# Attention kernel on one core: the projections of the next unit issued as four single products at steps 6, 8, 11 and 13 of a head, with their preparation one to two steps later

## What is computed

```
q = x @ W_q ; k = x @ W_k ; v = x @ W_v
latent = (k + v) @ W_down_kv
k_rec, v_rec = latent @ W_up_k, latent @ W_up_v        # 16 heads of 16
scores = q_h @ k_rec_h.T / sqrt(256) * decay           # decay = exp(-0.01 |t - s|)
out = softmax(scores) @ v_rec_h                        # for 2 x 16 heads, 2048 x 2048 each
x = x + layernorm(out @ W_o)                           # then the experts
```

## Time and profile before

| | us |
|---|---|
| median of 3 runs | 1645.92 (1645.17 to 1649.04) |
| the profiled execution, its own time | 1644.78 |
| its span, first to last instruction | 1643.1 |
| TensorE busy | 1553.8 |
| ScalarE busy | 1121.3 |
| VectorE busy | 558.6 |

### The profile page before, as it was taken

How to read it: one execution, slowest core, us unless ns; L and a number is a source line. 1 busy time by engine, 2 the same in 40 slices (tenths; PEclk the granted TensorE clock), 3 DMA queues, 4 the chain that set the end, 5 groups by cost and what they waited for, 6 DMA issues and landing times. The chain is left out here.

```text
span 1643.1 us, 26430 instructions
## 1 busy us (share of the span) xinstructions
PE 1553.8 (95%) x8752; PEld 685.6 (42%) x8753; DVE 558.6 (34%) x1624; ACT 1121.3 (68%) x1330; POOL 58.6 (4%) x104
## 2 busy tenths in 40 slices
PE   7769999999999999999999999987999999999996
PEld 5523333333333333333333333333646556556554
DVE  5612323313323323223222122132453543444442
ACT  4459999999999999999999999982222223223210
POOL 1000000000000000000000000000000000000000
PEclk9879999999999999999999999997999999999998
DMA  7565664575466466456556446522010010001000
GB/s 190 206 145 130 165 129 128 134 157 130 118 156 147 109 147 161 112 129 161 107 134 143 95 104 132 119 51 78 27 39 13 26 38 13 26 15 37 1 13 15
DMA packets 105425, 163.42 MB, mean 99 GB/s; under 512 B 52080, under 2 KB 72304, under 8 KB 96928
## 3 DMA queue, kind: packets, MB, share of 16 engines
q1 hardware_dynamic: 105376, 162.83, 41.1%
HBM read 120.84 MB, written 41.94 MB: 99 GB/s over the span
## 5 line engine op out<-in xcount | busy, mean ns | idle before, releaser
L702 ACT ACTIVATE work<-ps 128x1024 f32<-128x1024 f32 x1024 | 951.3, 1084 | 68.9 <-DVE ps L536 36.4
L632 PE MATMUL ps<-work 128*32 128x512 f32 x4096 | 548.1, 607 | 0.0
L624 PE MATMUL ps<-Q_st,K_st 64*128 64x512 f32 (+3 forms) x2432 | 440.9, 430 | 43.0 <-ACT work L702 28.2
L624 PEld LDWEIGHTS ps<-Q_st,K_st 64*128 64x128 f32 x2432 | 230.9, 184 | 541.5 <-ACT work L702 450.5
L536 DVE TENSOR_TENSOR ps<-ps,small 128x128 f32<-128x128 f32 x512 | 153.5, 300 | 743.0 <-PE ps L624 741.4
L1816 PE MATMUL ps<-xT,stack 128*128 (+1 forms) x320 | 156.7, 612 | 1.5 <-PEq L455 1.5
L1824 PE MATMUL ps<-xT,stack 128*128 (+1 forms) x320 | 151.3, 595 | 0.0
L1839 PE MATMUL ps<-stack,work 128*128 128x256 f32 x640 | 141.3, 380 | 0.0
L1789 ACT ACTIVATE work<-ps 128x512 f32<-128x512 f32 x80 | 47.6, 595 | 135.4 <-PE ps L1816 135.3
L632 PEld LDWEIGHTS ps<-work 128*32 128x32 f32 x4096 | 80.9, 108 | 113.7 <-issue 87.7
L1839 PEld LDWEIGHTS ps<-stack,work 128*128 128x128 f32 x640 | 120.4, 190 | 16.0 <-issue 0.2
(11 more groups left out here) (115 smaller groups left out, 746.7 us busy)
## 6 DMA issues: line engine op xcount, KB each, us to landing
K_st<-halves_dram SPq DMA_DIRECT2D x256, 256.0 KB, 5.6
halves_dram<-work SPq DMA_DIRECT2D x64, 512.0 KB, 3.7
Q_st<-halves_dram SPq DMA_DIRECT2D x256, 128.0 KB, 5.6
work<-in_L_attn_x SPq DMA_DIRECT2D x16, 512.0 KB, 4.9
attn_dram<-work SPq DMA_DIRECT2D x16, 256.0 KB, 6.6
work<-attn_dram SPq DMA_DIRECT2D x8, 512.0 KB, 3.9
out<-work SPq DMA_DIRECT2D x8, 512.0 KB, 2.9
decay<-in_c_decay SPq DMA_DIRECT2D x8, 256.0 KB, 10.4
```

The source lines that it names most:

```text
L624: m = nc.tensor.matmul(ps[:, half_of(s, half) + c % 2, q0 % CH:q0 % CH + w], K_st[tile, par, a, s * P:(s + 1) * P], Q_st[tile, par, a, at: ...
L632: m = nc.tensor.matmul(ps[STRIP * c:STRIP * (c + 1), ACC + par], Vg[:, par, s], probs[:, probs_of(par, s), chunk(c)], start=s == 0, stop=s ...
L702: nc.scalar.activation(probs[:, probs_of(par, s), half * HALF:(half + 1) * HALF], src, ACT.Exp, scale=SCALE).then_inc(s_["exp_done"], 1)
```

## The change

The function `project` issues one product (k) per call. The four calls come after the scores of steps 6, 8, 11 and 13. Before, both products of a block came after those of step 7, and both of the other after those of step 11. The preparation of the first block is at steps 9 to 11 in place of 8 to 10; that of the second at steps 14, 15 and step 0 of the odd head in place of 12 to 14. No arithmetic is added or removed.

```diff
-                        if prep and par == 0 and s >= 8 and s < 11:
-                            prepare(s - 8, it % PPU, 0, 2 * it, idle)
-                        if prep and par == 0 and s >= 12 and s < 15:
-                            prepare(s - 12, it % PPU, 1, 2 * it + 1, idle)
+                        if prep and par == 0 and s >= 9 and s < 12:
+                            prepare(s - 9, it % PPU, 0, 2 * it, idle)
+                        if prep and par == 0 and s >= 14:
+                            prepare(s - 14, it % PPU, 1, 2 * it + 1, idle)
+                        if prep and par and s == 0:
+                            prepare(2, it % PPU, 1, 2 * it + 1, idle)
...
-            def project(at, which, bank):
-                for k in range(KD):
-                    m = nc.tensor.matmul(ps[:, bank], w_unit[:, which, k], xT[:, k, at:at + CH] if isinstance(at, int) else xT[:, k, bass.ds(at, CH)],
-                                         start=k == 0, stop=k == KD - 1)
-                m.then_inc(s_["proj_ps"], 1)
+            def project(at, which, bank, k):
+                x = xT[:, k, at:at + CH] if isinstance(at, int) else xT[:, k, bass.ds(at, CH)]
+                m = nc.tensor.matmul(ps[:, bank], w_unit[:, which, k], x, start=k == 0, stop=k == KD - 1, skip_group_check=True)
+                if k == KD - 1:
+                    m.then_inc(s_["proj_ps"], 1)
...
-                            if s == 7:
+                            if s == 6:
                                 wait(pe, "w", it + 1)
                                 if not first:
                                     wait(pe, "att_sb", n)
-                                project(at, 0, idle)
+                                project(at, 0, idle, 0)
+                            if s == 8:
+                                project(at, 0, idle, 1)
                             if s == 11:
                                 wait(pe, "proj_free", 2 * it + 1)
-                                project(at, 1, idle)
+                                project(at, 1, idle, 0)
+                            if s == 13:
+                                project(at, 1, idle, 1)
```

## The result

The changed kernel takes 1652.61 us (median of 11 runs, 1650.32 to 1656.45); the kernel before, on the same chip, 1645.92 (11 runs). The ratio is 1.0042, with a 95% interval of 1.0034 to 1.0050: slower by more than the measurement is uncertain. The forecast was 1652.0 in a range of 1645.0 to 1656.5. The profiled execution took 1651.72 us, 6.94 more than that of before, and its span is 1649.9.

What follows compares the result with a forecast made beforehand. ScalarE's exponentials were taken to set the pace, stopped by TensorE's projections. Terms of 0.24 + 0.09 + 0.18 = 0.51 us per pair, 12 pairs, add 6.1 us: 1652.0 us forecast, range 1645 to 1656.5.

Steps and rivals of the forecast that it cites:

- What bounds the kernel: Attention: ScalarE's exponentials set the pace, one per 0.906 us; projections on TensorE stop them, costing 3.57 us per pair of heads.
- An insertion costs 1.25 us: TensorE, one single product between scores: 0.86 us streaming plus 0.39 us switching, paid four times per pair instead of twice.
- B: Rival, within 0.3%: switching is partly per projection, an insertion costs 1.05 us; -3.5 us, 1642.4; chance 0.31.
- C: Rival, faster: a lone product's weight loads are pulled ahead, an insertion costs 0.86 us; -12.6 us, 1633.3; chance 0.09.
- First block +0.24: Even head, insertions after steps 6 and 8: ScalarE loses 2.22 us in place of 1.98 per pair.
- the 0.15 us of catching up: TensorE between insertions: products follow each other in 1.66 us, ScalarE needs 1.81, so TensorE gains 0.15 us per step.
- Second block +0.09: Even head, insertions after steps 11 and 13: ScalarE loses 1.82 us in place of 1.73 per pair.
- Head's end +0.18: Piece 1 behind step 15's mask makes the odd head's first mask 0.35 us late; 0.18 us per pair stays.
- The 0.35: Odd head's step 0 mask: 0.35 us late, as piece 1 takes 1.67 us and the next mask comes after 1.32.
- piece 1: First part of a block's preparation on VectorE, including the cast; forecast to fill 1.67 us from mask to mask.
- Piece 2 and the loads cost nothing: Odd head's start: piece 2 (1.22 us) delays a mask by a covered 0.06 us; later loads keep 11 us of cover.
- The sum: Per pair 0.24 + 0.09 + 0.18 = 0.51 us; over 12 pairs 6.1 us slower.

## Why the prediction was right

*What bounds the kernel.* ScalarE's exponentials, stopped by TensorE's insertions: right. Every run's median moved by 12 times what its pair moved, within 2.1 us; the loss at the low clock in head 0 alone differs by up to 1.5 us from trace to trace.

*An insertion costs 1.25 us.* Measured 1.24. The switching belongs to the two ends of an insertion and not to its middle, as read from the gaps: 1.24 less the 0.86 streamed leaves 0.38 us at each of the two insertions that are shown. The Trainium skill, TensorE: Matmul & The Clock Gate, Part 3, The mechanism, says in one place that a weight load runs beside matmuls only where its row group differs, and in another that one for the background weight buffer is pulled ahead too. The gap behind a projection fits the first. The trace also shows what only the second allows: within a block, products of the same 128 rows follow each other 0.43 us apart with their weight loads of 0.19 beside them. And half of the 0.38 is not in that gap but in the parted halves of scores. Rivals B at 1.05 and C at 0.86 us are out for the places of this change. But B's value is real at another place, between products and scores.

*First block +0.24.* Measured 0.29: (2.56 + 2.01 + 2.22 + 2.73) in steps 6 to 9 is 2.28 above plain steps, against 1.99. Slightly mis-sized: the 0.15 us of catching up was read at one step and is 0.10 at those in which the diagonal cuts the scores into a third piece.

*Second block +0.09.* Measured 0.12 (1.87 against 1.75), by the same.

*Head's end +0.18.* Measured 0.15 in the changed kernel (0.34 at step 15, less 0.19 at step 0), 0.10 by itself: the mask is late by 0.29 and 0.28 and not by 0.35, and the odd head's stop of 0.19 is gone. The 0.35 was a misreading of the earlier trace rows. The 1.67 us between its two masks were not the length of piece 1: the second mask waited for the scores of step 10, which had started at 374.97, and started 0.55 us behind them, as the mask at 388.22 does behind scores at 387.67. From the start of the cast to the next mask VectorE needs 0.60 us (389.83 - 389.23, and 388.05 - 387.45 without a split), not 0.67. Against this, the mask of step 15 starts 0.42 us behind exponential 30 in the changed kernel and 0.35 before, which was not forecast; the two errors offset each other in part. With the split in place the cast is worth 0.23, as moving it showed.

*Piece 2 and the loads cost nothing.* Right: the mask of step 1 started 1.33 us behind that of step 0 with ScalarE not stopped, and the last load of head 10 was issued at 403.72 in place of 398.41, and landed 7.5 us later, with head 10 at 420.34: 9 us of cover where 11 were forecast. Odd heads are otherwise 0.05 us longer, which was not forecast: 0.03 at step 5, 0.03 at step 15 (2.88 in place of 2.85). The 2.88 stands also in the runs with the first block split, with blocks split in one round and with whole blocks ahead of the scores, whose second block is prepared within the even head, so it does not hang on the late preparation. Its cause is open.

*The sum.* 0.51 us per pair forecast, 0.61 measured, 12 x 0.61 = 7.3 us. The medians say 6.7, and 1.0034 to 1.0050 of 1645.92 is 5.6 to 8.2 us, which holds both. Against the 6.1 of the forecast the pairs are off by 0.10 us each: 0.05 and 0.03 at the two blocks and 0.05 in the odd heads, less 0.03 at the head's end. That the median (1652.61 against 1652.0) lies closer than the pairs is luck.

## What to carry to other kernels

Splitting work that an engine is late with does not make it less late when, as here, the engine catches up by 0.1 us per step and the split pays 0.4 us of switching again. Look for the place where the engine already stands still (here the head's end, 0.8 us) or already switches (here between products and scores, where the two halves of scores stay together), and count what each other engine's queue has between two signals that are closer together there than elsewhere.

## What was not expected of the hardware

An insertion of two fp32 instructions over 128 rows costs 1.24 us between scores of 64 rows, and 1.06 between products of 128 rows by 32 columns and scores, with 0.86 streamed in both. The difference is that between two halves of scores that stand together (0.67 us) and two that are parted (0.43 each). And the gain of the cheaper place is 0.19 us a block where TensorE is behind, 0.02 at step 12 and 0.07 at step 10 where it waits for an exponential in each round.
